# An S5-style block on one NeuronCore: rotation matrices built in one product with coefficients per half, and a direct term that ScalarE writes into PSUM banks

## What is computed

```
g   = group_norm(x, 32 groups)                       # 3 channels a group
fx  = layernorm over the 96 channels(g) * g1 + b1    # per position
Bu  = B_bar fx                                       # 48 complex modes
xs  = scan:  state[l] = lam_bar * state[l-1] + Bu[l] # along the 256 positions
y   = 2 Re(C xs) + D * fx                            # D * fx is the "direct term"
y   = gelu(y) + fx
fy  = layernorm over the channels(y) * g2 + b2
z1, z2 = split(W_enc fy);  out = x + W_dec (z1 * gelu(z2)) + fy
```

## Time and profile before

| | us |
|---|---|
| median of 3 runs | 105.83 |
| the runs | 105.36, 105.83, 112.51 |
| the profiled execution, its own time | 105.32 |
| its span in the profile | 103.5 |
| PE busy | 93.3 |
| DVE busy | 70.9 |
| ScalarE (ACT) busy | 43.5 |
| POOL busy | 38.4 |

### The profile page before, as it was taken

The page is one execution under the profiler, slowest core; times in us unless marked ns, Lnnn a source line. Parts: engine busy times, 40 slices in busy tenths (PEclk is TensorE's granted clock), DMA queues, the critical chain, the costliest instruction groups (busy, mean ns, idle before and its releaser), DMA issues.

```text
span 103.5 us, 1484 instructions
## 1 busy us (share of the span) xinstructions
PE 93.3 (90%) x494; PEld 54.5 (53%) x494; DVE 70.9 (69%) x223; ACT 43.5 (42%) x94; POOL 38.4 (37%) x54
## 2 busy tenths in 40 slices
PE   5998769979999998798999999995999999999960
PEld 3675547745676654675666546573333532533320
DVE  1566996899972898665995032799950699994590
ACT  3430069999566301070361079163179322034200
POOL 7702278900199960000182000048991000495000
PEclk9999999999999999999999999999999999999996
DMA  2999100000000000000000000000000000550225
GB/s 69 229 251 218 53 3 0 6 0 0 0 0 3 0 6 0 0 0 0 0 3 0 0 0 6 0 0 0 0 0 0 0 0 0 158 152 0 55 77 173
DMA packets 3783, 3.79 MB, mean 37 GB/s; under 512 B 512, under 2 KB 3680, under 8 KB 3776
## 3 DMA queue, kind: packets, MB, share of 16 engines
q1 hardware_dynamic: 3520, 3.68, 13.8%
q10 hardware_dynamic: 256, 0.02, 0.2%
HBM read 2.12 MB, written 1.57 MB: 36 GB/s over the span
## 4 chain that ended last, share of the span: by engine, by line
PE 61%; DVE 22%; DMA 7%; issue 3%; SPq 2%; ACT 1%; DVEq 1%
PE ps L503 61%; DMA xs<-x_dram 7%; DVE rs L759 3%; DVE upper L763 2%; DVE fy L759 2%; DVE rs L764 2%; DVE rs L789 2%; DVE sq L759 1%; SPq L249 1%; DVE w L759 1%; DVE st L798 1%; DVE y L1033 1%; DVE fx L759 1%; DVE parts L759 1%; ACT y L459 1%
## 5 line engine op out<-in xcount | busy, mean ns | idle before, releaser
L349 POOL TENSOR_TENSOR y<-gl,fx 96x512 f32<-96x512 f32 x4 | 6.4, 1603 | 28.0 <-ACT gl L453 28.0
L503 PE MATMUL ps<-fy,mt 96*96 96x512 f32 x32 | 14.9, 599 | 1.3 <-DVE fy L759 1.3
L357 POOL TENSOR_TENSOR res<-fy,xs 96x512 f32<-96x512 f32 x8 | 10.7, 1357 | 11.6 <-DVE fy L759 11.5
L503 PE MATMUL ps<-wm 96*96 96x256 f32 x42 | 12.5, 452 | 1.2 <-DVE wm L1001 1.2
L459 ACT ACTIVATE y<-ps,vecs 96x512 f32<-96x512 f32 x8 | 5.5, 685 | 16.5 <-PE ps L503 16.5
L759 DVE SCALAR_TENSOR_TENSOR w<-ps,vecs,y 96x512 f32<-96x512 f32 x8 | 5.9, 743 | 7.4 <-ACT y L459 7.4
L503 PE MATMUL ps<-xs,pm 96*96 96x256 f32 x32 | 8.5, 393 | 1.6 <-DVE pm L847 1.6
L503 PEld LDWEIGHTS ps<-wm 96*96 96x96 f32 x42 | 7.9, 197 | 4.0 <-DVE wm L1001 1.2
L503 PEld LDWEIGHTS ps<-fy,mt 96*96 96x96 f32 x32 | 5.0, 163 | 8.7 <-issue 6.8
L895 DVE TENSOR_TENSOR Z<-Z,ps 96x240 f32<-96x240 f32 (+3 forms) x8 | 2.8, 354 | 9.2 <-PE ps L503 9.2
L453 ACT ACTIVATE gl<-ps,db 96x512 f32<-96x512 f32 x8 | 5.5, 683 | 8.4 <-PE ps L503 8.1
(11 more groups left out here) (122 smaller groups left out, 163.3 us busy)
## 6 DMA issues: line engine op xcount, KB each, us to landing
out_dram<-sq SPq DMA_DIRECT2D x7, 192.0 KB, 2.2
xs<-x_dram SPq DMA_DIRECT2D x3, 384.0 KB, 7.2
xs<-x_dram SPq DMA_DIRECT2D x2, 192.0 KB, 3.1
mt<-mats_dram SPq DMA_DIRECT2D x1, 338.6 KB, 7.8
out_dram<-sq SPq DMA_DIRECT2D x2, 96.0 KB, 2.1
mt<-mats_dram SPq DMA_DIRECT2D x1, 180.0 KB, 5.8
sm<-small_dram ACTq DMA_DIRECT2D x1, 8.6 KB, 2.7
cmask<-mask_dram ACTq DMA_DIRECT2D x1, 9.0 KB, 3.3
```

The costliest lines, as they stand in the source:

```text
L349: nc.gpsimd.tensor_tensor(yv[:, RT * i:RT * (i + 1), :], cols(gl, H, i).rearrange("c (b m) -> c b m", b=RT), cols(fx, H, i).rearrange("c ( ...
L357: nc.gpsimd.tensor_tensor(cols(res, H, i), cols(fy, H, i), xs[:, HB * H + 2 * i:HB * H + 2 * i + 2, :].rearrange("c n l -> c (n l)"), ALU. ...
L503: return nc.tensor.matmul(o, lhsT, rhs, start=start, stop=stop)
```

## The change

1. The identity and the swap matrix become one, `eye + swap`; in it, row r has a one in column r and in column r ± 48. One product of it with a coefficient for the left 48 columns and one for the right 48, per row and power, gives the whole rotation. `rot` (8 matrices) is one DVE instruction, `rotX` (6 matrices) one POOL instruction; `rotC`, `rotS` and ScalarE's `rotations` go. POOL computes the coefficient tables with masks 0/1 from the small input (`M0`, `M1`, `NM0`), DVE two of them (`F0`, `F1`). PE's product for `um` is one call a piece, not two.
2. PE: that product comes after the second sample of half 1 is centred, and all six others after it; the last warm-up (two calls) goes. The broadcast of half 0 has no centring calls in it any more.
3. ScalarE makes the two copies to `um` ahead of the bias, the squares and the values of half 1. DVE: five steps of `step_chain` in the gap of the second group norm, not two; two `pm` of half 1 by DVE and six by ScalarE (which stand where `rotations` did); all steps are done ahead of `rot`, and `inverse_sigma(0, 0)` stands behind `rot` with nothing in between.
4. POOL: `combine` waits for `inv_ready[0]` at 1 in place of `pm_ready`, and the last `yl` product also for `inv_ready[0]` at 2 (the second half's inverse deviations).
5. `direct(1, i)` for tiles 0 to 2 goes from PE. Ahead of `carried_outputs(0, i)` PE runs `open_bank(i)`, one bf16 call of 512 columns with `start=True` on `bank(1, i)`; it waits until `scan` has read that bank. ScalarE then writes D * fx into the bank (`direct_term`), in the order term 0, gelu 0, term 1, gelu 1, gelu 2, gelu 3, term 2. PE waits for it ahead of `local_outputs(1, i)`, which adds.
6. `doubling(1, i)` comes ahead of `center(0, i)`, the first one also ahead of the waits for `y2`.

```diff
-WARM = (12, 1, 4, 2, 2)
+WARM = (12, 1, 4, 2)
@@ helpers
+        def halves(t):
+            return t.rearrange("p n (h j) -> p n h j", h=2)
+        def pairs(n_mats):
+            return m(M_PAIR).rearrange("p (h j) -> p h j", h=2).unsqueeze(1).broadcast_to([96, n_mats, 2, 48])
+        def coefs(k, n_mats):
+            return tb[:, k:k + 2, 0:n_mats].rearrange("p h n -> p n h").unsqueeze(3).broadcast_to([96, n_mats, 2, 48])
@@ gpsimd
+            pool.wait_ge(sines_ready, 1)
+            nc.gpsimd.tensor_scalar(tbl(S1), tbl(SIN), s(M1), None, ALU.mult).then_inc(cos_ready, 1)
+            nc.gpsimd.tensor_scalar(tbl(S0), tbl(SIN), s(NM0), None, ALU.mult).then_inc(cos_ready, 1)
             pool.wait_ge(sines_ready, 2)
...
             nc.gpsimd.tensor_scalar(tbl(COS), tbl(CM1), 1.0, None, ALU.add).then_inc(cos_ready, 1)
-            nc.gpsimd.tensor_scalar(tbl(NSS), tbl(SIN), s(RHO), None, ALU.mult).then_inc(cos_ready, 1)
-            pool.wait_ge(cos_ready, 2)
+            pool.wait_ge(cos_ready, 3)
...
-            ts(tbl(SSG), tbl(SIN), s(NRHO), None, ALU.mult)
+            ts(tbl(A0), tbl(COS), s(M0), None, ALU.mult)
+            ts(tbl(A1), tbl(COS), s(M1), None, ALU.mult)
             settle()
+            tt(tbl(X0), tbl(A0), tbl(S1), ALU.subtract)
+            tt(tbl(X1), tbl(A1), tbl(S0), ALU.subtract)
...
-            pool.wait_ge(pm_ready, FIRST_PM + HB)
+            pool.wait_ge(inv_ready[0], 1)
...
-            combine(rotX, M_ID, tbl(XCO, NX), M_SW, tbl(XSI, NX), NX).then_inc(rotx_ready, 1)
+            nc.gpsimd.tensor_tensor(halves(rotX), pairs(NX), coefs(XC0, NX), ALU.mult).then_inc(rotx_ready, 1)
             pool.wait_ge(yl_ready, 1)
+            pool.wait_ge(inv_ready[0], 2)
@@ scalar
+            def direct_term(i):
+                act.wait_ge(opened, i + 1)
+                nc.scalar.activation(bank(1, i)[0:96, :], cols(fx, 1, i), ACT.Copy,
+                                     scale=s(DD)).then_inc(direct_ready, 1)
...
-            rotations()
+            for n in range(FIRST_PM, HB):
+                scale_centering(1, n)
-            group_bias(1)
-            squares(1, 0, 2)
-            centered_values(1, 0, 2)
-            squares(1, 2, 4)
             act.wait_ge(umat_done, 1)
...
+            group_bias(1)
+            squares(1, 0, 2)
+            centered_values(1, 0, 2)
+            squares(1, 2, 4)
             squares(1, 4, HB)
...
-            gelu_y(0)
+            direct_term(0)
+            gelu_y(0, lambda i: direct_term(1) if i == 0 else direct_term(2) if i == NT - 1 else None)
@@ tensor
+            def open_bank(i):
+                pe.wait_ge(w_local[1], RT * (i + 1) - 1)
+                mm(bank(1, i)[0:96, :], bcm[:, 0, :],
+                   bcm[:, :, :].rearrange("p n c -> p (n c)")[:, 0:TILE], stop=False).then_inc(opened, 1)
...
-            pe.wait_ge(vecs_ready, 1)
-            center_batch(1, 2)
-            center_batch(1, 3)
-            warm_up(WARM[4], bank(1, 2))
             pe.wait_ge(taken[0], HB)
             pe.wait_ge(bst_ready, 1)
-            pe.wait_ge(rot_ready, T + 1)
+            pe.wait_ge(rot_ready, 1)
             for part, first, last in ((2, 0, 5), (3, 5, 8)):
-                o = bank(0, part)[0:97, 0:96 * (last - first)]
-                mm(o, bst[:, :], rotS[:, first:last, :], stop=False)
-                last_mm = mm(o, bst[:, :], rotC[:, first:last, :], start=False)
+                last_mm = mm(bank(0, part)[0:97, 0:96 * (last - first)], bst[:, :], rot[:, first:last, :])
             last_mm.then_inc(umat_done, 1)
+            pe.wait_ge(vecs_ready, 1)
+            for n in range(2, HB):
+                if n == 6:
+                    pe.wait_ge(bias_ready, 2)
+                center_batch(1, n)
             pe.wait_ge(bcm_ready, 1)
-            broadcast(0, 0, lambda: (center_batch(1, 4), center_batch(1, 5)))
-            pe.wait_ge(bias_ready, 2)
-            center_batch(1, 6)
-            center_batch(1, 7)
+            broadcast(0, 0)
...
             for i in range(NT - 1):
+                open_bank(i)
                 carried_outputs(0, i)
...
             for i in range(NT - 1):
-                direct(1, i)
+                pe.wait_ge(direct_ready, i + 1)
                 local_outputs(1, i)
                 if i == 0:
                     seed_sum(1)
-            pe.wait_ge(y2_pool, 2)
-            pe.wait_ge(y2_vec, 2)
             for i in range(NT):
+                doubling(1, i)
+                if i == 0:
+                    pe.wait_ge(y2_pool, 2)
+                    pe.wait_ge(y2_vec, 2)
                 center(0, i)
-                doubling(1, i)
@@ vector
-            group_norm(1, lambda j: step_chain_on(1), lambda: step_chain_on(2))
-            for n in range(3):
-                scale_centering(1, n)
-            dve.wait_ge(in_mats, 16)
-            dve.wait_ge(cos_ready, 2)
-            nc.vector.tensor_tensor(rotS[:, :, :], m(M_SW).unsqueeze(1).broadcast_to([96, T, 96]),
-                                    tbl(NSS, T).unsqueeze(2).broadcast_to([96, T, 96]),
-                                    ALU.mult).then_inc(rot_ready, 1)
-            inverse_sigma(0, 0, lambda j: scale_centering(1, j + 4) if j < 0 else step_chain_on(1))
-            for n in range(4, HB):
+            group_norm(1, lambda j: step_chain_on(1), lambda: step_chain_on(5))
+            for n in range(FIRST_PM):
                 scale_centering(1, n)
             for _ in steps:
                 pass
+            dve.wait_ge(cos_ready, 3)
+            par.add(stt(tbl(F0), tbl(COS), s(M0), tbl(S1), ALU.mult, ALU.add))
+            par.add(stt(tbl(F1), tbl(COS), s(M1), tbl(S0), ALU.mult, ALU.add))
+            par.settle()
+            nc.vector.tensor_tensor(halves(rot), pairs(T), coefs(F0, T), ALU.mult).then_inc(rot_ready, 1)
+            inverse_sigma(0, 0)
```

More of the change, by code:

```diff
@@ L76 @@
 RSQRT_SCALE = 64.0 / 9.0
-(LR, LI, LS, RHO, NRHO, G1, B1, DD, G2, B2, KV) = range(11)
+(LR, LI, LS, RHO, NRHO, G1, B1, DD, G2, B2, M0, M1, NM0, KV) = range(14)
 NS = KV + NK
-(M_NM, M_GD, M_GV, M_P, M_ID, M_SW, M_B, M_BS, M_C, M_CS, M_B1, M_WD, M_WE) = [96 * i for i in range(13)]
+(M_NM, M_GD, M_GV, M_P, M_ID, M_PAIR, M_B, M_BS, M_C, M_CS, M_B1, M_WD, M_WE) = [96 * i for i in range(13)]
 M_Z = M_WE + 192
@@ L85 @@
 NM = M_Z + ZW
-N_EARLY = M_SW
+N_EARLY = M_PAIR
 def s5_block(nc, x, small, mats, mask_in, out):
@@ L113, in s5_block @@
         mt = sb("mt", [96, NM])
-        rotC = sb("rotC", [96, T, 96])
-        rotS = sb("rotS", [96, T, 96])
-        rotX = sb("rotX", [96, 2, NX, 96])
+        rot = sb("rot", [96, T, 96])
+        rotX = sb("rotX", [96, NX, 96])
         bst = sb("bst", [96, C + 1])
@@ L159, in s5_block @@
         db_ready = sem("db_ready")
+        opened = sem("opened")
+        direct_ready = sem("direct_ready")
         w_full = sem("w_full")
@@ L220, in m @@
             return mt[:, c:c + n]
-        (ANG, XK, NRND, RED, EXM, TMP, SIN, SH, SH2, CM1, COS, SSG, NSS, RK, RSIN, CU, SU, XCO, XSI,
-         RSSG) = range(20)
+        (ANG, XK, NRND, RED, EXM, TMP, SIN, SH, SH2, CM1, COS, S0, S1, RK, RSIN, CU, SU, XC0, XC1,
+         A0, A1, F0, F1, X0) = range(24)
+        X1 = NRND
         (STEP, Y1, TH, RE, EXP, REC, NEG, T1, T2, T3, T4, CRE, CIM, DEN, ABSI, MASK, MR, MI, EXP1, REC1, POS) = range(21)
@@ L387, in sines, with scale_centering @@
                 nc.scalar.activation(tbl(SH), tbl(RED), ACT.Sin, scale=0.5).then_inc(sines_ready, 1)
[L389 to L400, removed]
+            def scale_centering(H, n):
+                act.wait_ge(gn_shift, H + 1)
+                nc.scalar.activation(pm[:, HB * H + n, :], m(M_P), ACT.Copy,
+                                     scale=gn[:, H, G_SCALE, n:n + 1]).then_inc(pm_act, 1)
             def group_bias(H):
@@ L446, in seed, with gelu_y @@
                     ACT.Copy).then_inc(z_seed, 1)
-            def gelu_y(H):
+            def gelu_y(H, between=lambda i: None):
                 act.wait_ge(db_ready, 1)
@@ L454, in gelu_y @@
                                          bias=db[:, 0:1]).then_inc(gl_ready, 1)
+                    between(i)
             def gelu_z(H, i):
@@ L462, in _ @@
             for n in range(FIRST_PM, HB):
-                scale_centering(n)
+                scale_centering(0, n)
             sines()
@@ L554, in variances, with broadcast @@
                     last.then_inc(variance[k], 1)
-            def broadcast(k, H, between=None):
+            def broadcast(k, H):
                 pe.wait_ge(inv_ready[k], H + 1)
@@ L561, in broadcast @@
                         pe.wait_ge(taken[0], HB * H + 2 * (i + 1))
-                        if H == 0 and i == 2:
-                            between()
                         if H == 0 and i >= 2:
@@ L589, in seed_sum @@
                 o = bank(H, NT - 1)[0:96, 0:RC].rearrange("p (n a) -> p n a", a=NA)
-                mm(o[:, :, 1:], rotX[:, 0, 0, :], w7[:, :, 0:NA - 1], stop=False)
```

(12 more changed lines are left out.)

17 lines of the change are left out of this document (8 added, 9 removed).

## The result

The changed kernel takes 102.25 us (median of 4; 101.41 to 108.92) where the kernel before took 105.59 beside it. The medians differ by 3.3 us. The ratio is 0.966, with an interval of 0.956 to 0.977, or 3.6 us; ratios leave out executions more than 1.5% above the fastest of their kernel. The forecast was 101.0, range 100.0 to 103.0. A second set of executions of the same kernel, in the first experiment, gave a median of 103.21 and a ratio of 0.974 (0.968 to 0.980). So the direction holds. The first median lies inside the range and the second 0.2 us above its end, and about a quarter of the 4.5 us that were forecast is missing.

The account below looks back on a forecast made before the run. PE was taken to bound the kernel, busy 93.3 of 103.5 us. Gains of 2.9 and 1.6 sum to 4.5: 105.32 becomes 100.8, plus 0.2 towards the runs' median gives 101.0 us; range 100.0 to 103.0.

Parts of the forecast that it names:

- PE's load, 2.15 us less: PE from 21 to 35 us: um product 1.29 instead of 2.58 us, and 0.86 of warm-up gone.
- When rot is there, 21.6: DVE after the second group norm's variance: 24 instructions at 0.13 us, 3.1 us; rot starts at 21.6, ends at 22.5.
- Rival A: DVE gives back the first part: POOL's longer tables delay rot and inverse_sigma, first broadcast 0.5 to 0.8 later; 101.9 us; chance 0.17.
- inverse_sigma undisturbed, 4.2: DVE's inverse_sigma(0, 0) behind rot: 4.2 us where it took 4.41 with strangers in it, ending at 26.7.
- From the broadcast to direct(0, 0), 5.7: PE after the first broadcast at 26.8: the old work remains, and direct(0, 0) starts at 32.5 instead of 34.94.
- The second broadcast, 3.0 earlier, taken as 2.9: PE and DVE meet at 38.7 and the 0.63 us wait goes; bounds 2.0 and 3.2.
- The second part, 1.6: Half 1's direct terms moved off PE, net 1.85 us, less a 0.25 wait in the last variances; bounds 0.6 and 1.9.
- the granted clock at full: A sign expected in the profile; a slice below nine tenths before the end would show the forecast wrong.
- Rival C: Slower: PE's gaps at 22.2 and 26.5 us drop the clock to 1.2 GHz; 9 us at that level gives 110; chance 0.04.
- B: ScalarE's ACTIVATE into PSUM takes 1.4 us, PE waits for term 2 and y2; about 1.5 lost, 102.5; chance 0.11.
- D: Second half: DVE's chain after variances sets the end and scan delays open_bank; 1.0 lost, 102.0 us; chance 0.08.
- theory C': Made for the experiments: PE's idle time from 20.3 to 22.6 us takes the clock to 1.2 GHz for some 3 us.

Follow-up runs that it names:

- the first experiment: The changed kernel run again with no edit, six executions beside the kernel before: median 103.21 us, ratio 0.974.
- early warm-up: Changed kernel with two more warm-up products in each of two gaps of the first group norm: four executions at 101.75 to 101.86 us, two at 104.1 and 104.3.
- ScalarE's terms alone: Kernel before with only opened banks, ScalarE's three direct terms, and doubling ahead of center: median 104.61 us, ratio 0.982.
- the yl experiment: Changed kernel in which POOL's last yl product does not wait for the second half's inverse deviations: median 105.50 us.
- rotations alone: Kernel before with only the rotations, the new order and POOL's waits; half 1's direct terms stay on PE, center ahead of doubling: median 104.84 us, ratio 0.989.
- last doubling: Changed kernel with its last two of doubling and center exchanged, center(0, 3) then doubling(1, 3): median 101.64 us.
- squares: Changed kernel with center(0, 3) ahead of doubling(1, 3), and ScalarE making tile 3's squares before tile 2's values: median 102.44 us.
- two steps: Changed kernel with two steps of step_chain in the second group norm's gap, not five: median 102.90 us.
- warm-up back: Changed kernel with the two removed warm-up products put back after half 1's second sample, before the product with rot: median 102.24 us, ratio 0.968.
- sample 2 first: Changed kernel with sample 2 of half 1 centred ahead of the product with rot: median 102.19 us, ratio 0.967.
- the two combined: Changed kernel with sample 2 ahead of rot's product, center(0, 3) ahead of doubling(1, 3), tile 3's squares first; without and with four early warm-up products: 101.30, 101.63 us.

## Why the prediction was right, and where it was off

- *PE's load, 2.15 us less*: right. At full clock the um product is 24.35 - 23.01 = 1.34.
- *When rot is there, 21.6*: wrong by 0.5. In the profile with the early warm-up rot starts at 21.91, or 22.11 on the scale of before, 0.25 later than rotS did. The step that failed is "26 instructions in 3.40 us, so 0.13 each". The group norm is a chain in which each instruction waits for the last; taking strangers out of it left it at 2.88 us (2.86 before). Only the pm and the steps behind it can be saved, and F0 and F1 came on top. With rot, inverse_sigma and the first broadcast came 0.5 later: 27.09 + 0.2 instead of 26.8. Rival A had this size, but by another mechanism: it wanted instructions on DVE to be held up by POOL, and the group norm's chain kept its 2.88 us beside POOL's longer list.
- *inverse_sigma undisturbed, 4.2*: right, both times (22.35 to 26.54 is 4.19).
- *From the broadcast to direct(0, 0), 5.7*: 6.04 at full clock. The squares of half 1, queued on ScalarE behind the copies of um, made the three variances take 0.20 us longer; that wait was left out. The other 0.14 is in the sum: the same work took 5.84 (28.19 to 34.03) where nothing in it waited. PE's 6.15 from direct(0, 0) on, in turn, were 6.03.
- *The second broadcast, 3.0 earlier, taken as 2.9*: 2.4 at full clock, from these items. The waits for yl and direct_ready that would have shown the forecast wrong did not come.
- *The second part, 1.6*: 1.58. The opened banks held PE for 0.22, 0.22 and 0.26, 0.70 in all where 0.73 was taken (47.91 to 48.13 for the first). ScalarE's term, an ACTIVATE that writes PSUM, took 0.69 against the 0.68 taken from its reading neighbours. The 0.25 us wait in the variances came, and most of it for the reason given; ScalarE's queue, which lay 0.08 behind it, was left out.
- *The clock.* This step failed: "the granted clock at full", with no term for it in the sum. By the prediction's own signs it is wrong if the clock shows a slice below nine tenths before the end, and both profiles of the changed kernel show such slices. Rival C had the place and the level (a fall to 1.2 GHz behind the gap at 22 us) and was wrong in being all or nothing: I asked whether 4.5 us would be lost and gave it 0.04. What happens is a fall of 3.4 us that costs 1.34, or one of 6.8 us, in a part of the executions. It should have been a term of the sum with a chance of its own. That the first median stays inside the range is luck as far as the clock goes: the range was made for A, B, D and the sizes, and the eleven executions of the changed kernel together have a median of 103.08, just outside it.
- *The share outside the span.* Own time less span was 1.82 us in the profile of before and 1.75 to 2.20 in 36 of its executions, and 1.80 to 2.12 with ScalarE's terms alone. In 71 executions of the kernels with the new rotations it is 2.14 to 2.38 in 53 and 2.80 to 3.42 in the other 18. The sum took it as fixed; it costs 0.2 us always and another 0.9 in about a quarter of the executions. What it is stays open: nothing outside the span is in the trace, and no experiment was made on it.

The sum again: 2.4 + 1.6 = 4.0 at full clock, which is the span's 103.3 to 99.3; less 0.2 outside it is 3.8, as in the two best executions of the first set (101.41 and 101.79 against 105.4). The executions with the short fall lose another 1.3, and the median, 102.25, lies between the two kinds.

**The clocks of all executions**, to judge theory C'. The profiles show three kinds of fall: a short one of 3.4 us (23.4 to 26.8 at a mean clock of 0.974, 23.1 to 26.5 at 0.983), a longer one from 22.8 to 29.6 (0.961, in the profile of the yl experiment), and one that begins in the first group norm, near 12 us (0.904). So an execution with a mean of 0.983 can have the short fall too, and the line between with and without is drawn at 0.99.

| below 0.99 | executions | of these at 0.903 to 0.908 |
|---|---|---|
| idle time before rot (the changed kernel, rotations alone, last doubling, early warm-up, squares, yl, two steps) | 28 of 47 | 5 |
| it is filled (warm-up back, sample 2 first, the two combined) | 4 of 24 | 0 |
| the kernel before, with a warm-up there | 19 of 36 | 5 |

The filled kernels ran on two chips, and on these two the kernels with the idle time had 14 of 24, two of them at 0.904. So filling it goes with fewer falls, as theory C' has it, but not with none. Six executions don't settle it for one kernel: on one chip the changed kernel had five of six below 0.99, and the one with the last doubling exchanged, whose first 58 us are the same, one of six. Only one execution of each kernel has a trace, so where the other falls begin is read from the mean alone. The kernel before has a warm-up there and falls about as often as those with the idle time. So a warm-up by itself is no guarantee, and why the filled kernels do better than it stays open.

The Trainium skill, "TensorE: Matmul & The Clock Gate", What's actually happening, has it that throttled is the default state and activity lifts it. The rows agree in part. The clock fell behind two idle times of 0.69 and 0.27 us and came back in a stretch in which PE was busy throughout (23.4 to 26.8 us). But it had stayed full behind the 0.97 us idle up to 13.48 in the same trace, so idle time alone does not say where it falls.

## What to carry to other kernels

Work removed from the bounding engine may leave idle time there, and in a part of the executions the granted clock then falls and takes some of the gain back. So before a warm-up goes, look for real work that can stand in its place, give the fall a chance of its own in the forecast, and read the granted clock in stretches of a microsecond, as busy time hides a half clock. A chain of small dependent instructions is priced by its waits, not by counting what stands between them (9 or 12 here). When reordering the bounding engine gives nothing although it waits, read the queue of the engine it waits for: two limits may lie close together, and only moving both gives the gain.

## What the runs showed of the hardware

- The same kernel has executions with and without a fall of TensorE's clock, so its times cluster. For the changed kernel: 101.4 to 102.1 at 0.99 or more, 102.7 to 103.3 at 0.973 to 0.983, 105.0 at 0.962, 109 at 0.904.
- A bf16 call of 512 columns held PE for 0.22 us where an fp32 call holds it for 0.86, and PE then added fp32 products to what ScalarE had written there in between. That makes a cheap call enough to let another engine start a sum.
- An ACTIVATE that reads SBUF and writes PSUM took 0.69 us for 96x512, about as long as one that reads PSUM and writes SBUF (0.68).
